# A graph layer's node stage: TensorE waits for its products and places itself, four groups of places in PSUM instead of three, lane numbers in SBUF

## The chip, the cores and the metric

The kernel runs on one core of a Trainium2 chip. The metric is the device time of one execution in microseconds, as a median of several runs. The engines are named as in the profile: PE is TensorE (PEld its weight loads), DVE is VectorE, ACT is ScalarE, POOL is GpSimd, SP is SyncE. A "q" behind a name (DVEq, PEldq) is that engine's sequencer, which loads registers, waits and issues DMAs.

## The reference

One graph layer over 50,000 nodes and 25,000 edges, 256 features each, everything in float32. The edges come sorted by their target node, and most point at low node numbers (the target is 50,000 times a uniform number squared).

```
h     = relu(layernorm(x))
msg   = relu(h[src] + edge_attr)                       # one row for each edge
p     = msg @ W_fc.T + b_fc
score = p @ Q.T                                        # 4 heads
alpha = softmax of score over the edges of one target node, for each head
pooled[n, head] = sum over the edges of n of alpha * p
gate  = softmax(mean over the edges of n of p @ Wg.T + bg)
out   = x + sigmoid(sum over the heads of gate * pooled)
```

In the end every edge has one weight, and a node's row is the weighted sum of its edges' rows of p, then a sigmoid, then x is added.

## The kernel before

The five engines run five instruction streams, written by hand, which meet at semaphores. There are three stages.

**Edge stage** (0 to 353 us of the profile). 196 tiles of 128 edges: POOL gathers the source rows (line 443), DVE and ACT do the layer norm and add the edge rows, PE turns and multiplies, and DVE writes the rows of p to `p_keep` in SBUF. Of the 196 tiles 64 are spilled to HBM and reloaded later by SP (line 394).

**Weights** (353 to 401 us). DVE and POOL work out one weight for each edge by scans over 128 x 256 tiles (lines 1132 to 1242, POOL's at lines 449 to 467). PE selects them by step (line 811) into PSUM banks 7 and 6, and DVE copies them to `wgt` in SBUF (lines 1264 and 1271).

**Node stage** (401 to 733 us), which the change is about. The 50,000 nodes are 391 blocks of 128, each a *place* of 256 columns in PSUM. A *step* is one pair (edge tile, node block): there are 196 + 391 - 1 = 586 of them. For each step DVE builds a 128 x 128 matrix in `spread` that has the edge's weight where the edge's target is the lane's node (line 1248), and PE multiplies it with the tile's rows of p into the block's place (line 829, two matmuls in the trace for each step). Four blocks are a *group*, the unit of everything behind PE; there are 98 groups. For each group:

- ACT waits until the group's last step is done, takes the sigmoid of its 128 x 1024 places into one of four buffers `yout` (line 597), writes zeros to the places (`clear`, line 573) and increments `zeroed`. Then it waits for POOL's sum of the group before, issues that group's store (line 605), and issues a load of x rows (line 552) in three groups of four.
- POOL adds the x rows to `yout` in place (line 478, 128 x 1024, both operands in SBUF) and issues the load of x for every fourth group itself (line 482).

PSUM holds 12 places, three groups, in banks 0 to 5: `POS = 12`, `SLOTS = 3`. Bank 7 holds the *lane numbers*, a 128 x 128 table that every spread is compared with (written once by line 1050).

Steps go in halves of six (`HALF`), and `spread` has 12 places (`AHEAD`), so DVE is at most 12 steps ahead of PE: `spreads` begins with a wait on `stepped`, the count of finished steps (PE adds 12 to it at the start). Before each half DVE also calls `need` (line 1252 and on): it loads a word of a table and waits for two counts, `p_ready` (tiles of p that are in SBUF again) and `zeroed` (groups whose places were cleared) as far as the *last* step of the half needs them. PE itself waits only for `spread_ready`, at every third step. PE's sequencer loads the 12 addresses of a half into registers (line 819).

Of the kernel before, what the change touches and what calls it, by code (L numbers as in the profile page):

```python
# [27 lines left out]
P = 128  # L28
# [6 lines left out]
def gnn_layer(nc, x, src, dst, edge_attr, w_fc, b_fc, q_w, g_w, b_g, out):  # L35
# [47 lines left out]
    WORDS = 2 * HALF  # L83
    HALVES = -(-STEPS // HALF)
    THREES = -(-(N // (GROUP * P)) // 3)
    POS = 12
    SLOTS = POS // 4
    assert STEPS % HALF and HALF % 3 == 0 and STEPS + AHEAD < 1024 and GROUPS < 128 and POS <= 16
    assert all((j * 683) >> 13 == j // POS for j in range(NODES))
    assert COLS == HALVES * HALF and TILES - P <= COUNT_ROW and THREES * 3 <= P  # L90

    FULL = N // (GROUP * P)
# [12 lines left out]
    with ExitStack() as ctx:  # L105
        def sb(name, shape, dt=F32):
            return ctx.enter_context(nc.sbuf_tensor(name, shape, dt))
# [25 lines left out]
        eps = sb("eps", [P, 1])  # L133
        bg_b = sb("bg_b", [P, H])
        column = sb("column", [P, P], I32)
        tab = sb("tab", [P, 48])
        tab_i = sb("tab_i", [P, 48], I32)
        next_i = sb("next_i", [P, BLK, 2], I32)
# [352 lines left out]
        def _(act):  # L491
# [83 lines left out]

            nc.scalar.activation(eps[:, 0:1], zero[:, 0:1], ACT.Sigmoid)
            act.wait_ge(rows_read, 1)
            for z in range(SLOTS):
                clear(z)
            act.wait_ge(words_in, 64)  # L580
            act.wait_ge(wgt_ready, 1)
            o_rows = out[0:FULL * GROUP * P, :].rearrange("(t p) d -> p t d", p=P)
            last_row = (FULL * GROUP + LAST_WHOLE) * P

# [81 lines left out]
        def _(pe):  # L666
# [148 lines left out]
            places = bank[:, :, :].rearrange("p b n -> p (b n)")  # L815
            p_rows = p_keep[:, :, :].rearrange("p t d -> p (t d)")

            def steps(half, s0, k0, n, apart=3):
                _, words = nc.values_load_multi_w_load_instructions(
                    path_of[:, bass.ds(half * WORDS, WORDS)], engines=[mybir.EngineType.PE], min_val=0,  # L820
                    max_val=(RING + STAGE) * T, skip_runtime_bounds_check_because=bound_by_shape)
                for k in range(n):
                    if k % apart == 0:
                        pe.wait_ge(spread_ready, s0 + k0 + min(k + apart, n))
                    p_at = nc.s_assert_within(words[k], 0, (RING + STAGE - 1) * T,
                                              skip_runtime_bounds_check_because=bound_by_shape)
                    place = nc.s_assert_within(words[HALF + k], 0, (POS - 1) * T,
                                               skip_runtime_bounds_check_because=bound_by_shape)
                    nc.tensor.matmul(places[:, bass.ds(place, T)], spread[:, k0 + k, :], p_rows[:, bass.ds(p_at, T)],  # L829
                                     start=False, stop=True, skip_group_check=True).then_inc(stepped, 1)  # L830
# [7 lines left out]
                    steps(2 * turn + h, turn * AHEAD, h * HALF, HALF)  # L838
            s0 = TURNS * AHEAD
            steps(2 * TURNS, s0, 0, HALF)  # L840
            steps(2 * TURNS + 1, s0, HALF, STEPS - s0 - HALF)


        @block.vector
        def _(dve):
            steps = [0]

            def then(ins):

                steps[0] += 1  # L850
                ins.then_inc(dve_step, 1)
                dve.wait_ge(dve_step, steps[0])
# [24 lines left out]
            def table_work(k):  # L877
# [45 lines left out]
                    v.tensor_tensor(node_nj, step_nj, tile_nj, ALU.subtract).then_inc(table_step, 1)  # L923
                elif k == 28:
                    dve.wait_ge(table_step, 17)
                    v.tensor_scalar(place_nj, node_nj, 683.0, None, ALU.mult).then_inc(table_step, 1)
                elif k == 29:
                    dve.wait_ge(table_step, 18)
                    v.tensor_copy(floor_nj, place_nj).then_inc(table_step, 1)
# [71 lines left out]
            def node_work(k):  # L1001
                b = k % 2
                blk = slice(b * P, (b + 1) * P)
                if k == 60:
                    v.memset(joins[:, 0:RW + 1:P], 0.0).then_inc(node_step, 1)
                elif k == 62:
                    v.tensor_tensor(per_blk(same)[:, :, 1:P], dst_f[:, :, 1:P], dst_f[:, :, 0:P - 1], ALU.is_equal
                                    ).then_inc(node_step, 1)
                elif k == 64:
                    dve.wait_ge(node_step, 3)  # L1010
                    v.tensor_scalar(neg, joins, 1.0, BIG, ALU.subtract, ALU.mult).then_inc(node_step, 1)
                elif k == 66:
                    v.tensor_tensor(cm, next_f[:, :, :], dst_f[:, :, 0:P:P - 1], ALU.is_equal).then_inc(node_step, 1)
                elif k == 68:
                    v.tensor_tensor(one_node, dst_f[:, :, 0], dst_f[:, :, P - 1], ALU.is_equal).then_inc(node_step, 1)
                elif k == 70:
                    dve.wait_ge(node_step, 6)
                    v.tensor_tensor(wc, cm, for_b(one_node), ALU.mult).then_inc(node_step, 1)
                elif k == 72:
                    dve.wait_ge(node_step, 7)  # L1020
                    v.tensor_copy(keep_cols, for_k(wc, C)).then_inc(node_step, 1)
                elif k == 74:
                    v.tensor_scalar(cneg, cm, 1.0, BIG, ALU.subtract, ALU.mult).then_inc(node_step, 1)
                elif k == 76:
                    v.tensor_scalar(wneg, one_node, 1.0, BIG, ALU.subtract, ALU.mult).then_inc(node_step, 1)
                elif k in (78, 79):
                    v.tensor_tensor_scan(in_first[:, blk], same[:, blk], ones[:, :], 0.0, ALU.mult, ALU.add
                                         ).then_inc(node_step, 1)
                elif k in (82, 83):
                    dve.wait_ge(node_step, 12)  # L1030
                    v.tensor_tensor_scan(less[:, blk][:, ::-1], same_next[:, blk][:, ::-1], in_first[:, blk][:, ::-1], 0.0,
                                         ALU.mult, ALU.max).then_inc(node_step, 1)
                elif k == 86:
                    dve.wait_ge(node_step, 14)
                    v.tensor_copy(count_at, per_blk(less)[:, :, 0:P:P - 1]).then_inc(node_step, 1)
                elif k in (88, 89):
                    dve.wait_ge(node_step, 15)
                    v.reciprocal(less[:, blk], less[:, blk]).then_inc(node_step, 1)
                elif k == 92:
                    dve.wait_ge(node_step, 17)  # L1040
                    v.tensor_scalar(less, less, -1.0, None, ALU.mult).then_inc(node_step, 1)
                elif k in (94, 95):
                    v.tensor_scalar(in_first[:, blk], dst_f[:, b, :], dst_f[:, b, 0:1], None, ALU.is_equal
                                    ).then_inc(node_step, 1)
                elif k in (96, 97):
                    v.tensor_scalar(in_last[:, blk], dst_f[:, b, :], dst_f[:, b, P - 1:P], None, ALU.is_equal
                                    ).then_inc(node_step, 1)
                elif k == 100:
                    dve.wait_ge(rows_copied, PARTS + 2)
                    v.tensor_scalar(bank[:, 7, P:2 * P], column[:, :], dst_0, None, ALU.subtract).then_inc(node_step, 1)  # L1050

            def measure(t):
                m, n = t % BODY, rows_of(t)
# [191 lines left out]
            def spreads(s0, k0, n):  # L1245
                dve.wait_ge(stepped, s0 + k0 + n)
                for k in range(k0, k0 + n):
                    v.tensor_scalar(spread[:, k, :], bank[:, 7, P:2 * P], rel[:, bass.ds(s0 + k, 1)],  # L1248
                                    wgt[:, bass.ds(s0 + k, 1)], ALU.is_equal, ALU.mult).then_inc(spread_ready, 1)

            def need_word(n):
                return dve.value_load(needs_of[:, bass.ds(n, 1)], min_val=257, max_val=(1 << 15) - 1)  # L1252

            def need(n):
                word = need_word(n)
                dve.wait_ge(p_ready, word & 255)
                dve.wait_ge(zeroed, word >> 8)

            dve.wait_ge(words_in, 64)
            first, second = need_word(0), need_word(1)  # L1260
            dve.wait_ge(p_ready, first & 255)
            dve.wait_ge(zeroed, first >> 8)
            dve.wait_ge(wgt_summed, 1)
            then(v.tensor_copy(wgt[:, 0:P], bank[:, 7, 2 * P:3 * P]))
            dve.sem_inc(wgt_ready, 1)
            spreads(0, 0, HALF)
            dve.wait_ge(p_ready, second & 255)
            dve.wait_ge(zeroed, second >> 8)
            spreads(0, HALF, HALF)
            dve.wait_ge(wgt_summed, 2)  # L1270
            then(v.tensor_copy(wgt[:, P:STEPS], bank[:, 6, 0:STEPS - P]))
            with dve.Fori(1, TURNS) as turn:
                for h in range(2):
                    need(2 * turn + h)
                    spreads(turn * AHEAD, h * HALF, HALF)
            s0 = TURNS * AHEAD
            need(2 * TURNS)
            spreads(s0, 0, HALF)
            dve.wait_ge(p_ready, TILES)
            dve.wait_ge(zeroed, GROUPS)  # L1280
            spreads(s0, HALF, STEPS - s0 - HALF)

            slot = (FULL - 1) % 4
# [35 lines left out]
```

## Time and profile before

| | us |
|---|---|
| median of three runs | 739.03 |
| the three runs | 735.18, 739.03, 739.16 |
| the profiled execution, its own time | 734.6 |
| its span, first to last instruction | 732.9 |
| mean granted TensorE clock | 0.946 |

The profiled execution's own time is 1.7 us more than its span, and 0.6% under the median. Over the whole span PE is busy 75%, DVE 67%, POOL 62%, ACT 52%. These shares are means over three stages with different limits, so the node stage has to be read by itself.

### The profile page before, as it was taken

What the parts mean: (1) busy time and instruction counts of PE and PEld (TensorE: products, weight loads), DVE (VectorE), ACT (ScalarE), POOL (GpSimd) and SP (SyncE); (2) the same over time, 40 slices, a digit from 0 to 9 for tenths busy, and PEclk for the clock granted to TensorE, in tenths of its full rate; (3) what the DMA queues carried; (4) which work ended last, traced back from release to release, by engine and by line L of the source; (5) the groups of instructions that cost most, each with busy time, mean ns of one, the idle gap of its engine ahead of it and who ended that gap; (6) DMA issues with size and microseconds to landing.
All of it is one profiled execution on the core that took longest, in us unless ns stands there. A gap on an engine that the chain in (4) does not pass through costs nothing.

```text
span 732.9 us, 12416 instructions
## 1 busy us (share of the span) xinstructions
PE 548.9 (75%) x2474; PEld 434.1 (59%) x2475; DVE 487.6 (67%) x1644; ACT 383.3 (52%) x661; POOL 453.4 (62%) x339
## 2 busy tenths in 40 slices
PE   2417988878779868879403998888888778877785
PEld 2205876666558656758202876776667566665564
DVE  4208678788879768769798766666565655555555
ACT  2105455656457545647211254666666666666674
POOL 7765565665560656550053366777877887778785
PEclk9999899999999999989855999999999999999999
DMA  7434455555553468775300799999999999999999
GB/s 223 131 93 134 147 173 174 165 174 154 174 170 114 129 224 271 237 234 191 115 0 1 247 355 383 314 307 329 357 319 329 325 327 339 325 337 336 341 333 332
DMA packets 137238, 171.53 MB, mean 234 GB/s; under 512 B 10096, under 2 KB 123784, under 8 KB 137202
## 3 DMA queue, kind: packets, MB, share of 16 engines
q10 hardware_dynamic: 91344, 90.23, 37.6%
q1 hardware_dynamic: 33010, 42.70, 18.6%
q0 software_dynamic: 12848, 38.20, 16.5%
q8 instruction: 12, 0.20, 0.1%
q14 instruction: 24, 0.20, 0.1%
HBM read 111.50 MB, written 59.60 MB: 233 GB/s over the span
## 4 chain that ended last, share of the span: by engine, by line
PE 52%; issue 12%; ACT 11%; DVE 10%; another core or an unknown queue 5%; ACTq 4%; DVEq 3%; POOL 2%; DMA 2%; POOLq 0%; SPq 0%
PE bank L745 24%; PE bank L829 18%; PE bank L735 7%; ACT arena L597 5%; DVE spread L1248 3%; ACT bank L573 3%; POOL arena L478 2%; ACTq L600 2%; DVEq L1252 1%; ACT arena L505 1%; ACTq L552 1%; ACTq L605 1%; ACT arena L497 1%; DMA p_keep<-p_spill 1%
## 5 line engine op out<-in xcount | busy, mean ns | idle before, releaser
L829 PE MATMUL bank<-p_keep,spread 128*128 x1172 | 274.1, 388 | 51.6 <-DVE spread L1248 46.7
L829 PEld LDWEIGHTS bank<-p_keep,spread 128*128 128x128 f32 x1172 | 219.0, 192 | 107.5 <-issue 79.8
L1248 DVE TENSOR_SCALAR spread<-bank,rel,wgt 128x128 f32<-128x128 f32 x586 | 195.8, 404 | 128.5 <-PE bank L829 72.8
L478 POOL TENSOR_TENSOR arena<-arena 128x1024 f32<-128x1024 f32 x96 | 224.9, 2352 | 73.1 <-ACT arena L597 72.7
L745 PE MATMUL bank<-w_all,arena 128*128 128x264 f32 (+1 forms) x784 | 228.0, 417 | 53.2 <-ACT arena L505 40.2
L745 PEld LDWEIGHTS bank<-w_all,arena 128*128 128x128 f32 (+1 forms) x784 | 143.7, 204 | 78.9 <-ACT arena L505 50.9
L597 ACT ACTIVATE arena<-bank 128x1024 f32<-128x1024 f32 x97 | 99.2, 1023 | 139.3 <-PE bank L829 120.3
L443 POOL DMA_INDIRECT p_keep<-in_x_dram,idx x124 | 120.8, 975 | 72.6 <-issue 31.5
L505 ACT ACTIVATE arena<-bank 128x256 f32<-128x256 f32 x196 | 73.6, 376 | 124.2 <-PE bank L735 71.0
L443 POOL DMA_INDIRECT arena<-in_x_dram,idx x72 | 70.1, 973 | 64.7 <-ACT arena L497 33.7
L573 ACT ACTIVATE bank<-zero 128x1024 f32<-128x1024 f32 x98 | 100.5, 1026 | 3.0
L735 PE MATMUL bank<-ident,arena 128*128 128x128 f32 x392 | 80.5, 289 | 24.4 <-DVE arena L1061 11.3
L735 PEld LDWEIGHTS bank<-ident,arena 128*128 128x128 f32 x392 | 56.8, 149 | 53.2 <-DVE arena L1061 13.5
L1061 DVE TENSOR_TENSOR arena<-arena 128x256 f32<-128x256 f32 x196 | 79.8, 408 | 6.7 <-issue 3.9
L497 ACT ACTIVATE arena<-p_keep,negmr,rstd 128x256 f32<-128x256 f32 x124 | 73.6, 594 | 20.3 <-issue 14.1
L1075 DVE TENSOR_TENSOR p_keep<-bank,bias 128x512 f32<-128x512 f32 x97 | 66.0, 680 | 0.0
L1073 DVE TENSOR_TENSOR logits<-bank,bias 128x16 f32<-128x16 f32 x97 | 16.5, 170 | 64.7 <-PE bank L745 34.6
L1055 DVE BATCH_NORM_STATS2 stats<-p_keep 128x6 f32<-128x256 f32 x124 | 51.7, 419 | 1.0 <-DMA p_keep<-in_x_dram,idx 0.6
L497 ACT ACTIVATE arena<-arena,negmr,rstd 128x256 f32<-128x256 f32 x72 | 42.7, 593 | 9.5 <-DVE negmr L1099 7.5
L1055 DVE BATCH_NORM_STATS2 stats<-arena 128x6 f32<-128x256 f32 x72 | 30.2, 419 | 0.0
L449 POOL TENSOR_SCALAR arena<-arena 128x1024 f32<-128x1024 f32 x1 | 3.9, 3852 | 42.5 <-DVEq L1183 42.5
L482 POOL DMA_DIRECT2D arena<-in_x_dram x24 | 18.6, 773 | 17.6 <-POOL arena L478 14.8
(202 smaller groups left out, 190.6 us busy)
## 6 DMA issues: line engine op xcount, KB each, us to landing
out_dram<-arena ACTq DMA_DIRECT2D x97, 512.0 KB, 4.5
arena<-in_x_dram ACTq DMA_DIRECT2D x73, 512.0 KB, 5.4
arena<-in_edge_attr_dram SPq DMA_DIRECT2D x48, 512.0 KB
arena<-in_x_dram POOLq DMA_DIRECT2D x24, 512.0 KB, 5.8
p_spill<-p_keep SPq DMA_DIRECT2D x16, 512.0 KB
p_keep<-p_spill SPq DMA_DIRECT2D x16, 512.0 KB, 5.8
p_keep<-in_x_dram,idx POOLq DMA_INDIRECT x124
arena<-in_x_dram,idx POOLq DMA_INDIRECT x72
```

What stands on the lines that cost most here:

```text
L443: pool.indirect_dma_start(out=x_row(t), out_offset=None, in_=x, in_offset=bass.IndirectOffsetOnAxis(ap=idx[0:rows_of(t), t:t + 1], axis=0) ...
L478: pool.tensor_tensor(yout[:, slot, :, :], yout[:, slot, :, :], xin[:, slot, :, :], ALU.add).then_inc(summed, 1)
L497: nc.scalar.activation(u[0:n, t % 4, :], x_row(t), ACT.Relu, bias=negmr[0:n, m:m + 1], scale=rstd[0:n, m:m + 1]).then_inc(ln_done, 1)
L505: nc.scalar.activation(msg_t[:, t % 4, :, 0:n], bank[:, TURNS_IN[t % len(TURNS_IN)], 0:D].rearrange("p (c e) -> p c e", c=KD)[:, :, 0:n], ...
L573: nc.scalar.activation(bank[:, 2 * z:2 * z + 2, :], zero[:, 0:1].unsqueeze(2).broadcast_to([P, 2, 512]), ACT.Copy).then_inc(zeroed, 1)
L597: nc.scalar.activation(yout[:, k % YS, :, :], places(k % SLOTS, GROUP), ACT.Sigmoid).then_inc(sig_done, 1)
L735: last = nc.tensor.transpose(bank[:, TURNS_IN[t % len(TURNS_IN)], c * P:c * P + n], u[0:n, t % 4, c * P:(c + 1) * P], ident[0:n, 0:n])
L745: last = nc.tensor.matmul(bank[0:n, 2 + t % 4, 0:NT], msg_t[:, t % 4, c, 0:n], w_all[:, c, :], start=(c == 0), stop=(c == KD - 1))
L829: nc.tensor.matmul(places[:, bass.ds(place, T)], spread[:, k0 + k, :], p_rows[:, bass.ds(p_at, T)], start=False, stop=True, skip_group_che ...
L1055: v.bn_stats(stats[0:n, m, :], x_row(t)).then_inc(stats_done, 1)
L1061: v.tensor_tensor(u[0:n, t % 4, :], u[0:n, t % 4, :], ea[0:n, t % BODY, :], ALU.add).then_inc(added, 1)
L1248: v.tensor_scalar(spread[:, k, :], bank[:, 7, P:2 * P], rel[:, bass.ds(s0 + k, 1)], wgt[:, bass.ds(s0 + k, 1)], ALU.is_equal, ALU.mult).th ...
```

## The change

1. PSUM holds 16 places, that is four groups, in all eight banks. The factor that computes the place of a step changes with it.
2. Banks 6 and 7 are now places too. The lane numbers move to a new SBUF tile `lane`, and every spread reads them there. ACT clears the fourth group of places after DVE has copied the last weights out of banks 6 and 7.
3. DVE no longer loads words and waits for `p_ready` and `zeroed`. PE's sequencer does both, at the start of each half, after it has loaded the half's addresses.

```
-    POS = 12
+    POS = 16
...
+        lane = sb("lane", [P, P])
...
-            for z in range(SLOTS):
+            for z in range(SLOTS - 1):
                 clear(z)
             act.wait_ge(words_in, 64)
-            act.wait_ge(wgt_ready, 1)
+            act.wait_ge(wgt_ready, 2)
+            clear(SLOTS - 1)
...
+            def held(half):
+                word = pe.value_load(needs_of[:, bass.ds(half, 1)], min_val=257, max_val=(1 << 15) - 1)
+                pe.wait_ge(p_ready, word & 255)
+                pe.wait_ge(zeroed, word >> 8)
...
+                if last:
+                    held_last()
+                else:
+                    held(half)
                 for k in range(n):
...
-                    v.tensor_scalar(bank[:, 7, P:2 * P], column[:, :], dst_0, None, ALU.subtract).then_inc(node_step, 1)
+                    v.tensor_scalar(lane[:, :], column[:, :], dst_0, None, ALU.subtract).then_inc(node_step, 1)
...
-                    v.tensor_scalar(spread[:, k, :], bank[:, 7, P:2 * P], rel[:, bass.ds(s0 + k, 1)],
+                    v.tensor_scalar(spread[:, k, :], lane[:, :], rel[:, bass.ds(s0 + k, 1)],
                                     wgt[:, bass.ds(s0 + k, 1)], ALU.is_equal, ALU.mult).then_inc(spread_ready, 1)
...
-            def need(n):
-                word = need_word(n)
-                dve.wait_ge(p_ready, word & 255)
-                dve.wait_ge(zeroed, word >> 8)
...
             with dve.Fori(1, TURNS) as turn:
                 for h in range(2):
-                    need(2 * turn + h)
                     spreads(turn * AHEAD, h * HALF, HALF)
```

## Rows read from the trace of the kernel before

**Rows 1.** Windows: us busy of PE, PEld, DVE, ACT, POOL (counts), granted clock, DMA share, GB/s.

```profile
440.00:460.00 20.00, 17.51 (x77) 13.96 (x76) 11.52 (x35) 10.26 (x10) 12.83 (x7) 1.00 1.06 382
...
500.00:700.00 200.00, 162.18 (x681) 127.29 (x681) 113.23 (x340) 128.96 (x127) 160.62 (x80) 0.98 1.02 333
```

**Rows 2.** Waits from 500 to 700 us: total, times, longest.

```profile
DVE spread L1248 <- ACT bank L573: 46.8, 24, 4.5
DVE spread L1248 <- PE bank L829: 39.7, 30, 3.8
```

**Rows 3.** The chain that ended last, around 630 us: start, us, what.

```profile
626.09 1.04 ACT bank L573
...
628.02 0.41 DVE spread L1248
...
628.58 2.81 PE bank L829 x8
631.41 1.03 ACT arena L597
```

**Rows 4.** Lines 478, 1248 and 482: shortest, median, longest in ns.

```profile
L478 POOL TENSOR_TENSOR arena<-arena x96: 2333/2351/2376, 412.2 to 724.5; 128x1024 f32<-128x1024 f32 x96
...
L1248 DVE TENSOR_SCALAR spread<-bank,rel,wgt x586: 397/402/414, 399.1 to 723.4; 128x128 f32<-128x128 f32 x196
...
L482 POOL DMA_DIRECT2D arena<-in_x_dram x24: 768/768/861, 414.9 to 717.3; - x24
```

**Rows 5.** Timeline where DVE and POOL both work on SBUF: start, us, instruction.

```profile
377.95 1.23 DVE L1191 TENSOR_TENSOR arena<-arena 128x1024 f32<-128x1024 f32 x1
377.96 2.34 POOL L452 TENSOR_TENSOR arena<-arena 128x512 f32<-128x512 f32 x1
...
379.31 1.04 DVE L1198 TENSOR_TENSOR logits<-logits 128x36 f32<-128x36 f32 x1
380.27 0.18 DVE L1199 TENSOR_TENSOR logits<-logits,spread 128x36 f32<-128x36 f32 x1
...
724.45 2.36 POOL L478 TENSOR_TENSOR arena<-arena 128x1024 f32<-128x1024 f32 x1 [0.76 <-ACT arena L597]
...
725.99 1.91 DVE L1286 TENSOR_TENSOR arena<-arena 128x1024 f32<-128x1024 f32 x1 [2.19 <-ACT arena L597]
```

**Rows 6.** Timeline: DVE's TENSOR_SCALAR from SBUF to SBUF, one beside a gather's issue.

```profile
193.30 0.28 DVE L1041 TENSOR_SCALAR spread<-spread 128x256 f32<-128x256 f32 x1
...
195.76 0.96 POOL L443 DMA_INDIRECT p_keep<-in_x_dram,idx  x1 [0.31 <-issue]
195.91 0.27 DVE L1043 TENSOR_SCALAR spread<-dst_f 128x128 f32<-128x128 f32 x1
...
392.87 0.47 DVE L1235 TENSOR_SCALAR arena<-arena,logits 128x128 f32<-128x128 f32 x2
```

**Rows 7.** Line 1248 in two stretches: us busy (count), clock, DMA share, GB/s.

```profile
412.20:500.00 87.80, 57.83 (x174) 1.00 0.98 333
500.00:727.00 227.00, 127.49 (x382) 0.98 1.02 335
```

**Rows 8.** Line 478 in the same two stretches.

```profile
412.20:500.00 87.80, 55.40 (x24) 1.00 0.98 333
500.00:727.00 227.00, 169.51 (x73) 0.98 1.02 335
```

**Rows 9.** Register loads of PE's and DVE's sequencers: shortest, median, longest in ns.

```profile
L819 PEldq TENSOR_LOAD <-path x98: 846/1697/3016, 397.1 to 722.7; - x98
...
L1252 DVEq TENSOR_LOAD <-few x97: 300/549/1474, 396.9 to 717.3; - x97
```

**Rows 10.** The chain from 401 to 446 us: start, us, what.

```profile
401.10 28.59 PE bank L829 x132
...
439.15 6.47 DMA p_keep<-p_spill
```

More of the change, by code:

```diff
@@ L85, in gnn_layer @@
     THREES = -(-(N // (GROUP * P)) // 3)
-    POS = 12
+    POS = 16
     SLOTS = POS // 4
     assert STEPS % HALF and HALF % 3 == 0 and STEPS + AHEAD < 1024 and GROUPS < 128 and POS <= 16
-    assert all((j * 683) >> 13 == j // POS for j in range(NODES))
+    assert all((j * 512) >> 13 == j // POS for j in range(NODES))
     assert COLS == HALVES * HALF and TILES - P <= COUNT_ROW and THREES * 3 <= P
@@ L816, in _, with held_last, steps @@
             p_rows = p_keep[:, :, :].rearrange("p t d -> p (t d)")
-            def steps(half, s0, k0, n, apart=3):
+            def held(half):
+                word = pe.value_load(needs_of[:, bass.ds(half, 1)], min_val=257, max_val=(1 << 15) - 1)
+                pe.wait_ge(p_ready, word & 255)
+                pe.wait_ge(zeroed, word >> 8)
+            def held_last():
+                pe.wait_ge(p_ready, TILES)
+                pe.wait_ge(zeroed, GROUPS)
+            def steps(half, s0, k0, n, apart=3, last=False):
                 _, words = nc.values_load_multi_w_load_instructions(
@@ L840, in _ @@
             steps(2 * TURNS, s0, 0, HALF)
-            steps(2 * TURNS + 1, s0, HALF, STEPS - s0 - HALF)
+            steps(2 * TURNS + 1, s0, HALF, STEPS - s0 - HALF, last=True)
         @block.vector
@@ L925, in table_work @@
                     dve.wait_ge(table_step, 17)
-                    v.tensor_scalar(place_nj, node_nj, 683.0, None, ALU.mult).then_inc(table_step, 1)
+                    v.tensor_scalar(place_nj, node_nj, 512.0, None, ALU.mult).then_inc(table_step, 1)
                 elif k == 29:
@@ L1247, in spreads @@
                 for k in range(k0, k0 + n):
-                    v.tensor_scalar(spread[:, k, :], bank[:, 7, P:2 * P], rel[:, bass.ds(s0 + k, 1)],
+                    v.tensor_scalar(spread[:, k, :], lane[:, :], rel[:, bass.ds(s0 + k, 1)],
                                     wgt[:, bass.ds(s0 + k, 1)], ALU.is_equal, ALU.mult).then_inc(spread_ready, 1)
-            def need_word(n):
-                return dve.value_load(needs_of[:, bass.ds(n, 1)], min_val=257, max_val=(1 << 15) - 1)
-            def need(n):
-                word = need_word(n)
-                dve.wait_ge(p_ready, word & 255)
-                dve.wait_ge(zeroed, word >> 8)
[L1259 to L1262, printed above, removed]
             dve.wait_ge(wgt_summed, 1)
@@ L1266, in _ @@
             spreads(0, 0, HALF)
-            dve.wait_ge(p_ready, second & 255)
-            dve.wait_ge(zeroed, second >> 8)
             spreads(0, HALF, HALF)
@@ L1271, in _ @@
             then(v.tensor_copy(wgt[:, P:STEPS], bank[:, 6, 0:STEPS - P]))
+            dve.sem_inc(wgt_ready, 1)
             with dve.Fori(1, TURNS) as turn:
                 for h in range(2):
-                    need(2 * turn + h)
                     spreads(turn * AHEAD, h * HALF, HALF)
             s0 = TURNS * AHEAD
-            need(2 * TURNS)
             spreads(s0, 0, HALF)
-            dve.wait_ge(p_ready, TILES)
-            dve.wait_ge(zeroed, GROUPS)
             spreads(s0, HALF, STEPS - s0 - HALF)
```

## The prediction

> **What bounds the kernel now.** I read the table of windows first, because the shares of the whole span mix three stages; the change touches only what runs after 399 us. From 500 to 700 us PE is busy 81%, POOL 80%, ACT 64%, DVE 57%, and the DMA engines' share is 1.02 [rows 1]. No compute engine is full, and the DMA queues nearly are: the share reached 1.06 from 440 to 460 us, with 382 GB/s against 333, but there the larger reload packets ran too. So transfers leave a little room (1.06 against 1.02, 4%) and no more.
>
> Next the waits. In those 200 us DVE idles 46.8 us until ACT has cleared places and 39.7 us until PE has done steps [rows 2]. The chain of waits shows the loop: clear at 626.09, spreads, first matmul at 628.58, the group's sigmoid at 631.41 [rows 3]. From clear to the end of that sigmoid are 6.35 us. A half of six steps asks for the places of its last step, so with three groups of places a group's steps can wait for the clear two groups back: 6.35 / 2 = 3.2 us for a group. The stage indeed takes 227 us for 73 sums of POOL [rows 8], 3.1 us each. The loop and the transfers (3.0 us for a group at share 1.06, see below) bound it together, and POOL with 2.35 us for a sum [rows 4] and 0.77 us for every fourth issue is third at 2.54 us.
>
> **Four groups of places, and the wait on PE.** The loop gets one group more: 6.35 / 3 = 2.1 us. It also loses DVE's part: from the end of the clear (627.13) to the first matmul (628.58) are 1.45 us [rows 3], which PE, with ready spreads, won't spend. So the 46.8 us of DVE's waits for clears stop to matter, and something else is late next. If only that were changed, it would be the transfers: a group now takes 227 / 73 = 3.11 us at share 1.02, and at 1.06 it would take 2.99. That is 0.12 x 73 = 9 us less. Waits for reloaded tiles (6.47 us of one are on the chain, [rows 10]) stay, but PE starts about 1 us sooner behind each of some three: 3 us less.
>
> **The register load on PE's queue.** PE's sequencer loads 12 addresses for each half, 0.85 us at the shortest [rows 9]. Now it loads one more word: on DVE that took 0.30 us at the shortest, 0.55 in the median [rows 9], plus some register work. Behind it are queued all six steps of the half. Where PE isn't the bound it costs nothing. Where PE is, from 401 us on, a step takes 28.59 / 66 = 0.433 us [rows 10], 2.6 us for a half; the sequencer runs ahead of the array, and 0.3 to 0.7 us may or may not fit. The bounds are 0 and 0.4 us for each of some 34 halves up to 500 us, 0 to 14 us. I take 0, since that stretch gets another bound, below.
>
> **The fourth clear.** 1.03 us of ACT near 404 us, where ACT waits until 411 for its first sigmoid: nothing. The changed factor, the write of the lane numbers and the waits of DVE that go: nothing, each is one instruction for one, or hidden by PE.
>
> **The lane numbers in SBUF.** This is the part that decides. Today a spread reads PSUM and writes SBUF. Its 586 executions took 397 to 414 ns, and POOL's 96 sums 2333 to 2376 ns [rows 4]: though both engines are busy most of the time, neither ever lengthens the other. Where DVE and POOL both read two operands of SBUF, the rows look different. POOL's 128 x 512 sum took 2.34 us, as long as a 128 x 1024 one: it was started 0.01 us after a DVE instruction of 1.23 us and ended 1.13 us behind it, half of 2.35. In turn DVE's 128 x 36 operation took 1.04 us until POOL had ended, where the next of its size took 0.18 [rows 5]. And in the node stage itself the last sum but one, DVE's 128 x 1024 at 725.99, took 1.91 us instead of 1.23, beside POOL's line 478 [rows 5]. They exclude each other, one whole instruction at a time.
>
> Will the new spread be of that kind? A TENSOR_SCALAR from SBUF to SBUF took 0.28 us for 256 columns and 0.27 for 128; two in a row took 0.47, so one follows the other by 0.20 us [rows 6]. 256 columns in 0.28 us is about twice the pace of DVE's sums (1.23 us for 1024, [rows 5]), so it uses a second way into SBUF. I therefore expect a spread to get shorter, 0.20 us each in a row instead of 2.0 / 6 = 0.33, and to wait for POOL's sum or make it wait.
>
> The Trainium skill says the same of the mechanism (SBUF — State Buffer, section "Who interferes with whom": a tensor_scalar in a two-port mode and any GpSimd instruction lock each other out for the whole instruction, while one with a PSUM source does not). Its warning about descriptors (same page, section "SBUF: two separate sides") goes further: a DMA issued from GpSimd starves while DVE is in such a mode. Row against rule: the gather's issue at 195.76 took its usual 0.96 us and line 1043 inside it 0.27 [rows 6], so neither was held. By the rule each of POOL's 24 issues could be held by six spreads, 1.2 us, 29 us more; by the row, nothing.
>
> The sum for the time in which the two exclude each other, with 2.35 us for a sum and 0.20 for a spread:
> - 412 to 500 us: 24 x 2.35 + 174 x 0.20 = 56.4 + 34.8 = 91.2 us, now 87.8 [rows 7, 8].
> - 500 to 727 us: 73 x 2.35 + 382 x 0.20 = 171.6 + 76.4 = 248.0 us, now 227.
>
> That is 3.4 + 21.0 = 24.4 us more, if one of the two always has work and all spreads that can do so lie beside POOL's 24 issues. If none does, 24 x 0.77 = 18.5 us come on top [rows 4]: 42.9. The bounds: +24.4 and +42.9, taken +33.6, the middle, since POOL's issue comes right behind a sum, when DVE is waiting. In a late group this is 2.35 + 5.2 x 0.20 + 0.1 = 3.5 us, over the transfers' 2.99, so the 9 us above are not had. The 3 us behind reloads are. Sum: +30.6 us. From the profiled time, 734.6 + 30.6 = 765; it stood 0.6% under the median, so the median of the new kernel should be 765.2 x 739.03 / 734.6 = 769.8; I say 769.
>
> What is queued behind a spread that waits: DVE's next ones, up to 2.35 us late. PE then has at most six spreads left, 2.6 us of work, so it should mostly not run dry; who waits is POOL, and behind it ACT, which issues a store only when the sum is done.
>
> **Rivals.**
> 1. *The exclusion costs only the streaming part, and the gains pay for it.* If a spread holds the way only 0.14 us (half of the 0.28 for 256 columns), 556 x 0.06 = 33 us fall off: -12 to +7 us around now, time 727 to 746, no change within what can be told. For it: in a row, DVE instructions overlap by 0.07 us. Against it: the 1.13 us behind the DVE instruction show nearly no overlap.
> 2. *Faster: the spread doesn't exclude POOL* (its two per-partition operands keep it in the slow form, or it fits into POOL's idle 20%). Then transfers decide: -9 - 3 = -12 us, 734.6 - 12 = 722.6, as a median 727. The point from which it decides: a late group has 2.99 - 2.35 = 0.64 us beside the sum, so a spread must cost under 0.64 / 5.2 = 0.12 us of POOL's time. For it: POOL idles 20%. Against it: each engine's work must then fall into the other's gaps by itself, and POOL's sums already follow closely.
> 3. *Slower still.* A spread alone takes 0.27 us, and if POOL and DVE alternate one by one, none overlaps: 556 x 0.07 = 39 us more, 805; or PE, waiting more, is granted a lower clock, or its sequencer's 14 us show. One of these in part: 780 to 805.
>
> That the change doesn't do what it says is hardly open: the wait for clears on DVE will be gone; rival 2 is the case where only that part works.
>
> **How the numbers follow.** Forecast 769 (752 to 779): 0.60. Rival 1: 0.15. Rival 2: 0.11. Rival 3: 0.14. A measurement of this kernel tells about 1% from no change, 731.6 to 746.4. Slower by over 1%: 0.60 + 0.14 and a sliver of rival 1 = 0.75; within 1%: 0.13; faster: 0.12. The range takes in the forecast, rival 1's upper half and rival 3's lower: 735 to 790.
>
> **What the new profile would show.** Line 1248 with lengths from 0.27 to above 2 us instead of 402 ns throughout, and line 478 from 2.35 to about 3.5; DVE's idle time until line 573 gone and PE waiting for spreads instead; POOL with the larger share, DMA share under 1.0 in the late windows; about 3.5 us for a group. The prediction is wrong if line 478 still has one length, if spreads take 402 ns, or if the stretch of PE at 401 us is longer than 0.433 us for a step.

## The result

| | before | after |
|---|---|---|
| median, us (4 runs each) | 739.1 | 810.76 |
| lowest to highest, us | 735.18 to 740.42 | 804.60 to 816.87 |
| profiled execution, us | 734.6 | 804.6 |
| its span, us | 732.9 | 802.9 |

The ratio of after to before is 1.0951, with an interval of 1.0867 to 1.1036: 9.5% slower, where 4% was forecast (769 us, range 735 to 790). The ratio leaves out the run of 816.87 us, which is over 1.5% above the fastest of its kernel and stands in the median.

The lines that decide, from the summaries of lines 479, 483 and 1263 in the profile after (POOL's sum, its issue of a load of x, and the spread; shortest, median and longest in ns). They answer to [rows 4]:

```profile
L479 POOL TENSOR_TENSOR arena<-arena x96: 2334/2352/2488, 410.8 to 794.5; 128x1024 f32<-128x1024 f32 x96
...
L483 POOL DMA_DIRECT2D arena<-in_x_dram x24: 766/766/872, 413.5 to 783.9; - x24
...
L1263 DVE TENSOR_SCALAR spread<-lane,rel,wgt x586: 328/335/5422, 397.4 to 794.5; 128x128 f32<-128x128 f32 x196
```

POOL's sums kept their 2.35 us. A spread is quicker at its shortest (328 ns against 397) but takes up to 5.4 us. So the two do exclude each other, and nearly all the waiting is DVE's. The timeline of after, at 655 us, shows one such spread, and at 662 us a worse one:

```profile
655.61 2.35 POOL L479 TENSOR_TENSOR arena<-arena 128x1024 f32<-128x1024 f32 x1 [1.71 <-ACT arena L599]
...
655.93 2.11 DVE L1263 TENSOR_SCALAR spread<-lane,rel,wgt 128x128 f32<-128x128 f32 x1 [0.66 <-PE bank L844]
...
662.50 0.77 POOL L483 DMA_DIRECT2D arena<-in_x_dram  x1 [0.68 <-POOL arena L479]
...
662.60 5.44 DVE L1263 TENSOR_SCALAR spread<-lane,rel,wgt 128x128 f32<-128x128 f32 x2
...
663.29 4.66 POOL L479 TENSOR_TENSOR arena<-arena 128x1024 f32<-128x1024 f32 x2
```

The first starts inside a sum and ends 0.08 us behind it (658.04 against 657.96). In the second, two sums run back to back to 667.95, and the second of two spreads ends at 668.04, behind both. This spread starts at 662.86, 0.43 us before the first of the two sums, but inside POOL's issue of 662.50. All eight spreads that took over 5 us in this kernel started inside such an issue: the issue holds a spread too, and the sums that come right behind it pass the one that waits.

The table of windows of after, then its waits from 500 to 700 us; before, [rows 1] and [rows 2]:

```profile
500.00:700.00 200.00, 145.25 (x577) 108.66 (x576) 182.34 (x290) 107.59 (x106) 134.41 (x66) 0.97 0.89 278
```

```profile
ACT arena L599 <- PE bank L844: 87.7, 48, 5.8
...
POOL arena L479 <- ACT arena L599: 55.1, 34, 4.3
PE bank L844 <- DVE spread L1263: 34.0, 24, 3.0
DVE spread L1263 <- PE bank L844: 18.2, 20, 3.5
PE bank L844 <- ACT bank L574: 15.3, 19, 1.7
```

DVE is "busy" 91% now, most of it with waiting inside a spread. DVE's wait for clears (46.8 us) is gone, and PE has one of 15.3 us in its place. POOL waits for ACT, ACT for PE, PE for DVE, and DVE for POOL: a ring in which spreads and sums don't overlap. The DMA share fell from 1.02 to 0.89.

The whole stage after 500 us fits the sum of what excludes each other. These are the windows of line 1263 and then of line 479, which answer to [rows 7] and [rows 8]:

```profile
412.20:500.00 87.80, 67.29 (x142) 0.98 0.86 275
500.00:796.00 296.00, 264.30 (x412) 0.95 0.87 273
```

```profile
412.20:500.00 87.80, 42.07 (x19) 0.98 0.86 275
500.00:796.00 296.00, 182.46 (x78) 0.95 0.87 273
```

How far apart unhindered spreads follow is seen before POOL's first sum, in the timeline of after from 397 us:

```profile
397.39 3.17 DVE L1263 TENSOR_SCALAR spread<-lane,rel,wgt 128x128 f32<-128x128 f32 x12
```

That is (3.17 - 0.33) / 11 = 0.258 us. 412 x 0.258 + 182.5 = 288.8 of the 296 us: in this stretch either a sum or a spread runs nearly all the time. Counted one by one in the trace, a sum or a spread (held ones with their waiting) is under way in 278.8 of the 296 us; the estimate is higher because a spread under way when a sum starts still runs into it for 0.1 to 0.2 us.

### The profile page after: what moved, and what is told of

Read it like the earlier page. It is cut to its first block, busy times and chain, and to the rows that moved or that the text cites. A ratio compares the mean times of both kernels' runs of the same rounds, so it can differ in the third digit from the quotient of the medians.

```text
span 802.9 us, 12416 instructions
## 1 busy us (share of the span) xinstructions
PE 573.8 (71%) x2474; PEld 440.3 (55%) x2475; DVE 633.6 (79%) x1643; ACT 383.5 (48%) x661; POOL 454.6 (57%) x339
## 4 chain that ended last, share of the span: by engine, by line
PE 43%; DVE 28%; issue 15%; another core or an unknown queue 6%; ACT 4%; DVEq 3%; DMA 1%; POOL 1%; ACTq 0%; SPq 0%
PE bank L844 19%; PE bank L747 18%; DVE spread L1263 15%; PE bank L737 4%; DVE p_keep L1090 2%; DVEq L1263 2%; DVE arena L1076 2%; DVE stats L1070 2%; ACT arena L599 1%; ACT bank L574 1%; DMA p_keep<-in_x_dram,idx 1%; ACT arena L498 1%; ACT arena L506 1%; DVE arena L1190 1%
## 5 line engine op out<-in xcount | busy, mean ns | idle before, releaser
L1263 DVE TENSOR_SCALAR spread<-lane,rel,wgt 128x128 f32<-128x128 f32 x586 | 342.5, 670 | 56.7 <-PE bank L844 55.6
L844 PE MATMUL bank<-p_keep,spread 128*128 x1172 | 295.1, 403 | 103.2 <-DVE spread L1263 73.0
L844 PEld LDWEIGHTS bank<-p_keep,spread 128*128 128x128 f32 x1172 | 224.7, 199 | 174.1 <-issue 145.0
L747 PE MATMUL bank<-w_all,arena 128*128 128x264 f32 (+1 forms) x784 | 230.7, 421 | 44.7 <-issue 16.6
```

The costliest lines, as they stand in the source:

```text
L747: last = nc.tensor.matmul(bank[0:n, 2 + t % 4, 0:NT], msg_t[:, t % 4, c, 0:n], w_all[:, c, :], start=(c == 0), stop=(c == KD - 1))
L1263: v.tensor_scalar(spread[:, k, :], lane[:, :], rel[:, bass.ds(s0 + k, 1)], wgt[:, bass.ds(s0 + k, 1)], ALU.is_equal, ALU.mult).then_inc(sp ...
```

## The experiments

Each was timed against runs of the kernel before on the same chip, and its ratio is to those. Diffs are against the kernel that is named.

**1. The lane numbers alone.** Against before:

```
-                    v.tensor_scalar(spread[:, k, :], bank[:, 7, P:2 * P], rel[:, bass.ds(s0 + k, 1)],
+                    v.tensor_scalar(spread[:, k, :], lane[:, :], rel[:, bass.ds(s0 + k, 1)],
```

> The kernel before with the lane numbers in SBUF and nothing else changed. Theory A (POOL's sums hold DVE's spreads off SBUF, and that is the whole loss): with one group of places less than the changed kernel and DVE's waits kept, at least as slow as it, 800 to 850 us, and about one spread in ten takes over 2 us. Rival B (the loss is PE's own waits: the word it loads and the clear it waits for): no loss here, 730 to 745 us, since spreads get shorter.

Measured: 805.48 us against 731.98, ratio 1.096 (1.090 to 1.103). Line 1249 of its profile is the spread:

```profile
L1249 DVE TENSOR_SCALAR spread<-lane,rel,wgt x586: 329/336/5174, 396.6 to 797.0; 128x128 f32<-128x128 f32 x196
```

One operand moved from PSUM to SBUF gives the whole loss of the change. Of the 586 spreads 52 took over 2 us, one in eleven, as theory A had it.

**2. PE's waits alone.** Against before: the wait part of the change, with twelve places and the lane numbers in PSUM.

```
+            def held(half):
+                word = pe.value_load(needs_of[:, bass.ds(half, 1)], min_val=257, max_val=(1 << 15) - 1)
+                pe.wait_ge(p_ready, word & 255)
+                pe.wait_ge(zeroed, word >> 8)
...
-                    need(2 * turn + h)
```

> The kernel before with the waits for products and places moved from DVE to PE, twelve places and the lane numbers in PSUM as before. Theory A: spreads keep 402 ns and POOL's sums 2.35 us; the loop over two groups loses DVE's part, so 725 to 740 us, at or a little under the kernel before. Rival B: 780 to 815 us, with PE's idle time behind its own sequencer.

Measured: 770.36 against 731.98 us, ratio 1.053 (1.048 to 1.059). Theory A gave 725 to 740 and missed. It wasn't all of the loss as rival B had it either: there is a second cost, which the changed kernel doesn't add to the first. The timeline of PE in this kernel, and then the one of the kernel before at a place where PE has its spreads in time:

```profile
602.98 2.85 PE L842 MATMUL bank<-p_keep,spread 128*128 x12 [0.75 <-DVE spread L1261]
606.99 1.34 PE L842 MATMUL bank<-p_keep,spread 128*128 x5 [1.15 <-DVE spread L1261]
```

```profile
477.68 6.64 PE L829 MATMUL bank<-p_keep,spread 128*128 x30
```

Here PE makes its 12 matmuls of a half and then idles; there it runs through the end of a half without a gap. The trace puts the idle time down to the spreads, but the wait that is longest in this kernel between 412 and 727 us is DVE's for PE:

```profile
DVE spread L1261 <- PE bank L842: 149.9, 83, 4.8
```

And counted in the trace, the third spread of a half was done over 0.4 us before the half's first matmul in all 97 halves behind the first. So the spreads lay ready.

**3. One way into SBUF.** Against after: the spread reads 3 x 43 lane numbers at a step of 44 and writes a run of 129 columns, the last of which isn't used.

```
-                    v.tensor_scalar(spread[:, k, :], lane[:, :], rel[:, bass.ds(s0 + k, 1)],
+                    v.tensor_scalar(spread[:, k, :].rearrange("p (a b) -> p a b", a=3), lane[:, :, 0:43], rel[:, bass.ds(s0 + k, 1)],
```

> The changed kernel, but a spread reads 3 rows of 43 lane numbers and writes 129 columns in one run (one column more than is used), which should keep DVE out of the form that reads SBUF by two ways. Theory A: every spread takes about 0.35 to 0.45 us, none waits for POOL, and sixteen places with PE's waits then show their own worth: 720 to 737 us, bound by the transfers (DMA share 1.0 or more). If the form is kept all the same, about 810 us as the changed kernel. Rival B: 780 us or more with spreads of one length.

Measured: 771.43 against 731.98 us, ratio 1.051 (1.045 to 1.058).

```profile
L1263 DVE TENSOR_SCALAR spread<-lane,rel,wgt x586: 393/399/411, 395.7 to 759.1; 128x129 f32<-128x129 f32 x196
```

The spreads are as expected, 399 ns and never held, with source and destination in SBUF. So it isn't SBUF as such but the faster form that collides with POOL. The time stays where PE's waits alone put it (770.36): with the collision gone, the second cost stands bare, and four groups of places win nothing beside it.

The Trainium skill's conditions fit: by SBUF — State Buffer, section "Who interferes with whom", an instruction with at most one SBUF input outside the two-port modes doesn't contend with GpSimd. VectorE: DVE Perf Modes, section "What auto-detection actually checks", wants the outermost dimensions of source and destination both even, or equal, for the two-port mode. 3 rows read against one run of 129 written is neither, and 399 against 335 ns agrees.

**4. POOL's sum made small.** Against after; the output lacks x in all but one element of each partition and group.

```
-                    pool.tensor_tensor(yout[:, slot, :, :], yout[:, slot, :, :], xin[:, slot, :, :],
+                    pool.tensor_tensor(yout[:, slot, 0, 0:1], yout[:, slot, 0, 0:1], xin[:, slot, 0, 0:1],
```

> The changed kernel, with POOL adding x to one element of each partition instead of 1024 (the output lacks x elsewhere). Theory A: POOL hardly holds SBUF, all spreads take about 0.33 us, 715 to 735 us, bound by the transfers. Rival B: 780 us or more, since PE's waits are all still there.

Measured, in two runs: 764.87 against 731.98 us, ratio 1.045 (1.037 to 1.053).

```profile
L1263 DVE TENSOR_SCALAR spread<-lane,rel,wgt x586: 327/342/648, 390.6 to 748.6; 128x128 f32<-128x128 f32 x196
```

The form is the quick one and the long waits are gone, so it is POOL's sum that holds the spreads. What is left of them shows the issue alone: 17 spreads took over 0.4 us, all beside one of POOL's 24 issues, and most of them ended about 0.03 us behind it. The time misses theory A's 715 to 735 by the same second cost as in 2 and 3.

**5. One way into SBUF, sixteen places, and the waits back on DVE.** Against experiment 3:

```
-                if last:
-                    held_last()
-                else:
-                    held(half)
...
+                    need(2 * turn + h)
```

> Sixteen places, lane numbers in SBUF read in the one-way form (3 x 43, 129 columns), but the waits for products and places back on DVE as before. Theory C (what PE's sequencer does at the start of a half, behind its load of twelve words, is bare: no matmul is left in its queue by then; about 0.9 us for each half) and A together: both costs are gone, so 715 to 735 us beside 732 for the kernel before, and here the fourth group of places shows what it is worth. Rival D (PE's wait for the clear itself costs, not the load, and more places cost something too): 745 us or more.

Measured: 717.81 against 733.70 us, ratio 0.979 (0.975 to 0.983). It beats both kernels. Its windows:

```profile
500.00:700.00 200.00, 167.45 (x699) 133.39 (x697) 115.57 (x351) 134.58 (x133) 169.82 (x85) 0.97 1.04 349
```

The DMA share is 1.04 and the rate 349 GB/s against 333, and no engine is busier than POOL with 85%. That points to transfers as what is left, as rival 2 of the prediction had it; no run takes transfers away to show it.

**6. Only the load.** Against before: PE loads the word of each half and doesn't use it; DVE still waits.

```
+                if not last:
+                    pe.value_load(needs_of[:, bass.ds(half, 1)], min_val=257, max_val=(1 << 15) - 1)
                 for k in range(n):
```

> The kernel before, and PE's sequencer also loads the word of each half, but doesn't use it: DVE still waits. Theory C: 750 to 770 us, most of the loss of the kernel with PE's waits alone (770 us), with one idle piece of PE of 0.5 to 0.9 us for each half. Rival D: 730 to 737 us, as before.

Measured: 767.14 against 733.70 us, ratio 1.045 (1.040 to 1.050), six sevenths of the cost in 2. So it is the load with its check that costs, and not the wait. Line 823 of its profile:

```profile
L823 PEldq FUSED_REGOPS  x191: 42/151/165, 395.2 to 754.4; - x191
L823 PEldq TENSOR_LOAD <-few x97: 301/306/1191, 394.9 to 753.4; - x97
L823 PEldq SEQ_ASSERT  x97: 18/18/24, 395.5 to 754.6; - x97
```

306 + 151 + 18 ns and the gaps between them are about 0.6 us for each half. The load of twelve words ahead of it takes 846 ns at the shortest but 1.7 us in the median [rows 9]. From 401 to 412 us, where PE is full, it takes 0.85 to 0.86 us in the kernel before, and nothing opens a gap there (in 2 PE is busy 12.59 of 13.20 us from 399). Later it takes up to 3.0 us, and then it ends only about when the last matmul of the half starts: in the median 0.31 us behind that start in the kernel before, and 0.07 us in this one (counted in the traces, as are the next figures). What makes it longer there is not shown. PE has nothing queued behind the load, so what the sequencer does from there to the first matmul delays PE. That stretch is 1.04 us in the median here and 0.30 in the kernel before. Of these 0.74 us for each half about half shows in the time (33 us over 97 halves, 0.34 us).

**7. One load of thirteen words.** Against experiment 3: the word is the thirteenth of its half's row, so the row has 13 words.

```
-        path = sb("path", [P, HALVES, WORDS], I32)
+        path = sb("path", [P, HALVES, WORDS + 1], I32)
...
-                    path_of[:, bass.ds(half * WORDS, WORDS)], engines=[mybir.EngineType.PE], min_val=0,
+                    path_of[:, bass.ds(half * (WORDS + 1), WORDS + 1)], engines=[mybir.EngineType.PE], min_val=0,
```

> As the run in the one-way form (771 us, sixteen places, PE waits), but the word that PE waits by comes as a thirteenth word of the load that is there anyway. Theory C: the second load (0.31 us) goes, its checks and shifts stay (0.4 to 0.5 us), so a third to a half of the loss goes: 745 to 762 us. Rival D: unchanged at 765 to 775 us.

Measured: 914.68 against 733.70 us, ratio 1.25 (1.24 to 1.26). Both theories missed. The load itself:

```profile
L829 PEldq TENSOR_LOAD <-path x98: 1105/3550/6057, 392.9 to 900.2; - x98
```

**8. Lane numbers and sixteen places, DVE's waits.** The changed kernel with `need` back on DVE, as in 5, and the spread in the plain form.

> The changed kernel with the waits back on DVE: sixteen places, lane numbers in SBUF in the plain form. Theory A: POOL's sums still hold the spreads, 780 to 805 us, near the kernel before with the lane numbers alone (805 us), a fourth group of places giving little. If PE's loads added to it one for one, it would be 770.

Measured: 803.92 against 733.70 us, ratio 1.097 (1.087 to 1.106). Beside 1 (1.096) the fourth group gives nothing, and beside the changed kernel (1.095) PE's load costs nothing. The summaries of the twelve-word load, first of after, then of experiment 5, differ:

```profile
L830 PEldq TENSOR_LOAD <-path x98: 845/858/2921, 395.9 to 792.2; - x98
```

```profile
L821 PEldq TENSOR_LOAD <-path x98: 846/1620/3551, 391.8 to 705.2; - x98
```

In the changed kernel half of the loads take nearly their shortest time, and so they do without PE's load (median 863 ns here, 862 in 1), so the second load is not what makes them short. What does isn't shown. The second load still delays PE at the start of a half: where the spreads were ready, 1.13 us lie between the start of one half's last matmul and of the next one's first in the changed kernel, and 0.22 here (medians, counted in the traces). But spreads and sums are what the time hangs on, and PE's idle time only changes its name: between 412 and 796 us it waits 72.2 us for spreads, 22.1 for clears and 7.6 for its own issue in the changed kernel, 102 in all, and 90.6 for spreads and 4.8 for its own issue here, 95 in all.

**9. The one-way form alone.** Against before: the spread of experiment 3, twelve places, DVE's waits.

> The kernel before with the lane numbers in SBUF in the one-way form, nothing else: twelve places, DVE waits. Theory A: no spread waits for POOL, so the same time as before, 728 to 738 us, and the 2.1% that the same form won together with sixteen places belongs to the places. If the form itself were the gain, about 718 us.

Measured: 733.07 us (10 runs) against 731.61 (13 runs), ratio 1.000 (0.996 to 1.004). The form is neutral, so the 2.1% of 5 are those of the fourth group of places.

**10. The sum in quarters.** Against experiment 8:

```
-                    pool.tensor_tensor(yout[:, slot, :, :], yout[:, slot, :, :], xin[:, slot, :, :],
-                                       ALU.add).then_inc(summed, 1)
+                    for part in range(4):
+                        ins = pool.tensor_tensor(yout[:, slot, part, :], yout[:, slot, part, :], xin[:, slot, part, :],
+                                                 ALU.add)
+                    ins.then_inc(summed, 1)
```

> Sixteen places, plain lane numbers in SBUF, waits on DVE (804 us), with POOL's sum of 128 x 1024 cut into four of 128 x 256. Theory A (one whole instruction at a time): DVE gets in between quarters, a held spread takes 0.6 to 0.9 us and none 2.4, and POOL's quarters get lengthened by spreads: 735 to 770 us. Rival E (POOL keeps SBUF over instructions that follow each other): spreads of 2.4 us stay, 795 to 815 us.

Measured: 813.53 against 731.61 us, ratio 1.109 (1.099 to 1.119): theory A missed. The timeline, and the summary of line 1252:

```profile
644.89 6.86 DVE L1252 TENSOR_SCALAR spread<-lane,rel,wgt 128x128 f32<-128x128 f32 x2
...
645.51 6.15 POOL L480 TENSOR_TENSOR arena<-arena 128x256 f32<-128x256 f32 x9
```

```profile
L1252 DVE TENSOR_SCALAR spread<-lane,rel,wgt x586: 329/343/8809, 395.0 to 800.0; 128x128 f32<-128x128 f32 x196
```

Nine quarters passed one waiting spread, and the longest spread took 8.8 us. So POOL can keep SBUF over instructions that follow each other closely, as rival E had it. It doesn't always: just before, from 640.2 to 645.6 us, a spread ended behind each quarter. Of the fifteen spreads over 5 us eleven started inside one of POOL's issues, but not this one, so what decides stays open. Cutting the sum into short instructions didn't help here.

**11. Rows of 13 words, twelve loaded.** Against experiment 5: the rows of the table are 52 bytes long instead of 48.

```
-                    path_of[:, bass.ds(half * WORDS, WORDS)], engines=[mybir.EngineType.PE], min_val=0,
+                    path_of[:, bass.ds(half * (WORDS + 1), WORDS)], engines=[mybir.EngineType.PE], min_val=0,
```

> The fastest kernel so far (718 us), with rows of 13 words instead of 12 in the table of addresses, still loading twelve. The load of thirteen words made the kernel slow (915 us), with loads of up to 6 us. Theory F (a load of twelve words is slow when its row doesn't begin at a multiple of 16 bytes or so): 850 to 930 us. Rival G (the thirteenth word itself is the cost): 715 to 722 us.

Measured: 859.29 against 731.61 us, ratio 1.174 (1.165 to 1.184), where 5 had 0.979.

```profile
L821 PEldq TENSOR_LOAD <-path x98: 851/3661/6997, 392.2 to 843.1; - x98
```

The same instruction with the same number of words has a median of 3.7 us instead of 1.6 once its rows begin at multiples of 52 bytes. Which of them, the trace shows, load by load: the 25 loads whose row begins at a multiple of 16 bytes in the table took 0.85 to 1.97 us, with a median of 0.86, and none of the other 73 took under 2.87. In 7 it is the same: 1.11 to 2.10 us for the 25, and no other under 3.10. So theory F held as it was told, with its 16 bytes.

**12. One load of thirteen words, rows of 16.** Against experiment 7: rows of 64 bytes.

> One-way lane numbers, sixteen places, PE waits, thirteen words in one load as in the slow run (915 us), but rows of 16 words, so that each row begins at a multiple of 64 bytes. Theory F: the 915 us go away. Theory C then gives what the run of thirteen words was made for: without the second load of 0.31 us and with the checks and shifts left, a third to a half of the 38 us of PE's waits is gone: 745 to 760 us. Rival D: 765 to 775 us. Rival G (the thirteenth word costs by itself): over 800 us.

Measured: 684.82 against 657.11 us, ratio 1.041 (1.035 to 1.047). Both kernels ran faster on this chip than on those of the other experiments, most of it ahead of the node stage (PE's first step is at 321.7 us, in 3 at 398.1), so the times themselves don't compare, only differences and ratios.

```profile
L829 PEldq TENSOR_LOAD <-path x98: 1097/1650/3362, 317.9 to 672.0; - x98
```

The 25% of 7 are gone, so they were the rows' beginnings and not the thirteenth word. (This kernel also puts the words that are waited for into the same tile as the addresses.) Of the cost of PE's waits 27.7 us is left from 39.5 in experiment 3: three tenths less, just under the third to a half that theory C gave. The percentages, 4.1 and 5.1, differ less because the whole time that they are shares of is shorter here. The shortest load went from 846 to 1097 ns, so a part of the 306 ns saved came back.

## Why the prediction was wrong

- *Where the loss sits.* Right: the lane numbers in SBUF alone give a ratio of 1.096, the whole change 1.095.
- *The exclusion, one whole instruction at a time* [rows 5]. Right for a spread behind a sum (experiments 1, 3, 4). In the other direction it was mis-told: a sum's longest is 2.49 us, so POOL waited for one spread at most. POOL's line didn't grow to 3.5 us; that it still has one length is one of the three signs that the prediction named for being wrong. Who waits is DVE and behind it PE (34.0 us for spreads from 500 to 700 us), which "should mostly not run dry".
- ***The step that failed is the size of the term "0.20 us for a spread".*** It was the spacing of an instruction with one per-partition operand [rows 6]; the spread has two and follows at 0.258 us. Over the 556 spreads of the sum that is 0.058 x 556 = 32 us more. With it the lower bound of the sum, +24.4, is +57; from 412 to 796 us the kernel after took 384 us against 314.8, that is +69. The profiled execution was 70 us slower, 31 were forecast, and 32 of the 39 missing are this term. That the second operand makes the difference between 0.20 and 0.258 is not shown; the two instructions also differ in their operations.
- *POOL's issues, 0 to 18.5 us, taken 9.* Right in size. 12 us remain of the 69. In the trace spreads run beside the first 0.4 us of an issue, and one that comes later is held to its end (experiment 4). As an estimate that is 24 x 0.34 = 8 us. The row that the prediction took for free passage [rows 6] is an instruction that began 0.15 us into a gather's issue and had ended by 0.42, so it says nothing of the later part. The rule that it set beside that row, issues held by spreads, didn't show: the issues kept 766 ns, and it is the spreads that wait.
- *Transfers out of the way, 9 us not had.* Right: DMA share 0.89. Whether the 3 us behind reloads were won, no run separates.
- *PE's second load, taken at 0 of 0 to 14 us.* Right for this kernel, and because of the other bound that it named (experiment 8). As a price it was far off: 38 us for the waits alone (2), 33 for the load without the wait (6). The sentence that the sequencer "runs ahead of the array" was right for the first stretch from 401 us, from which its 0.433 us for a step were read, and wrong behind 412 us, where the load of twelve words takes longer and its end is no longer ahead of the last matmul. Where the other bound is taken away, PE's second load costs 0.3 to 0.4 us for each half.
- *Four groups of places: 12 us less where nothing else is in the way* (rival 2, 727 us). Right in size once both costs are taken out: 717.81 against 733.70, 16 us (5), at a DMA share of 1.04. The share was taken to go from 1.02 to 1.06, and it went half of that way, so that the size comes out is in part luck.
- *Rival 3* had the failed term nearly right, with 0.07 us more for a spread, and gave 805 (809, had it been scaled to the median as the forecast was). Its reason, strict alternation, holds in part: a spread that comes during a sum is held, but unhindered ones follow each other as before.

## What to carry to other kernels

An operand's place is also a choice of the way in: moving one operand of a DVE instruction from PSUM to SBUF can switch it to a form that waits for POOL's instructions in SBUF and for its DMA issues. Before such a move count POOL's busy time beside it, and either leave one operand in PSUM or give the instruction a shape that keeps the slow form. Take the spacing for such a sum from an instruction with the same operation and operands. And what is put on PE's queue behind a load of registers delays its next matmul; with the same load and waits on DVE, which runs a half ahead, the kernel took 717.81 us instead of 771.43 (experiments 5 and 3).

## What the runs showed that I had not expected

- A register load on PE of twelve words whose rows begin at multiples of 52 bytes has a median of 3.66 us and reaches 7.0; at multiples of 48 bytes it is 1.62, of 64 bytes 1.65 with thirteen words. The kernel went from 0.979 to 1.174 of the time before by this alone. Within the run of 52 bytes only the rows that begin at a multiple of 16 bytes load fast (median 0.86 us), and every other takes at least 2.87.
- POOL can keep DVE out of SBUF over nine instructions of 0.7 us in a row.
- POOL's issue of a load (0.77 us) holds a spread in the fast form, and a spread held there can be passed by two sums of 2.35 us that start after it. In the slow form no spread took over 414 ns (the kernel before, experiment 3).
- The two costs of the change don't add: 9.6% and 5.3% alone, 9.5% together with a fourth group of places.
